# Four of the sixteen tiles of squares summed by TensorE instead of VectorE, in the two bfloat16 contractions of a four-layer kernel

## The reference

```python
z = layernorm(_gn(x), norm_w, norm_b)
left  = sigmoid(z @ w_lgate.T) * mask * (z @ w_left.T)
right = sigmoid(z @ w_rgate.T) * mask * (z @ w_right.T)
out = einsum(left, right) over k, for each of the 64 channels   # bfloat16 operands in layer 0
out = layernorm(out over the 64 channels, onorm_w, onorm_b)
x = x + (out @ w_out.T) * sigmoid(z @ w_ogate.T)
```

## Time and profile before

| | before |
|---|---|
| time, median of 3 runs | 2086.19 us (2081.47 to 2086.61) |
| time of the profiled execution | 2083.57 us |
| its span, first to last instruction | 2081.8 us |
| granted TensorE clock, mean | 0.964 |
| busy share PE / DVE / ACT / POOL | 89% / 81% / 76% / 29% |
| contraction of half 0 in the span | 265.13 to 306.46 us |
| contraction of half 1 in the span | 377.80 to 419.72 us |

### The profile page before, as it was taken

The page is one execution under the profiler, slowest core; times in us unless marked ns, Lnnn a source line. Parts: engine busy times, 40 slices in busy tenths (PEclk is TensorE's granted clock), DMA queues, the critical chain, the costliest instruction groups (busy, mean ns, idle before and its releaser), DMA issues. The chain is left out here.

```text
span 2081.8 us, 44989 instructions
## 1 busy us (share of the span) xinstructions
PE 1857.6 (89%) x14620; PEld 1249.0 (60%) x14620; DVE 1693.1 (81%) x2717; ACT 1585.0 (76%) x2204; POOL 602.0 (29%) x579
## 2 busy tenths in 40 slices
PE   5798979789888999989989899999997989999998
PEld 4324959555422777855632498987552248878554
DVE  6799989989689868778969896988775987777775
ACT  4698969769899657658989884876888976676676
POOL 1001919265200000016500290741871000000655
PEclk8899989999999999999999999999999999999999
DMA  9599938289789838269979984926997994864897
GB/s 395 226 314 298 250 82 242 81 306 358 306 268 332 301 122 295 69 242 384 418 251 313 280 220 127 282 77 252 392 419 250 311 321 165 273 204 152 298 366 316
DMA packets 297398, 549.55 MB, mean 264 GB/s; under 512 B 14768, under 2 KB 170416, under 8 KB 273712
## 3 DMA queue, kind: packets, MB, share of 16 engines
q1 hardware_dynamic: 295680, 538.38, 74.7%
q10 hardware_dynamic: 1584, 9.51, 1.1%
HBM read 371.67 MB, written 176.16 MB: 263 GB/s over the span
## 5 line engine op out<-in xcount | busy, mean ns | idle before, releaser
L1665 POOL TENSOR_TENSOR LR<-LR,sum 128x2048 f32<-128x2048 f32 x30 | 136.6, 4552 | 512.1 <-DVE LR L1458 512.1
L1674 POOL TENSOR_TENSOR LR<-LR 128x512 f32<-128x512 f32 x96 | 136.5, 1444 | 484.7 <-DVE LR L1720 468.9
L697 PE MATMUL bank<-LR,kst 128*128 128x512 f32 x512 | 252.5, 616 | 8.9 <-ACT LR L719 6.6
L897 POOL TENSOR_TENSOR msgs<-sigs,mask_sb 128x256 f32<-128x256 f32 x192 | 129.3, 689 | 393.0 <-ACT sigs L871 389.5
L1554 PEld LDWEIGHTS bank<-kst,LR 128*128 128x128 f32 x1024 | 152.0, 193 | 110.5 <-issue 89.3
L1566 PE MATMUL bank<-LR,wog 128*128 128x512 f16 x768 | 213.8, 388 | 4.8 <-ACT msgs L1621 4.0
L697 PEld LDWEIGHTS bank<-LR,kst 128*128 128x128 f32 x512 | 86.9, 189 | 178.9 <-issue 172.7
L1039 PE MATMUL bank<-LR 128*128 128x256 f32 x768 | 169.6, 383 | 7.0 <-DVE LR L936 4.2
L1554 PE MATMUL bank<-kst,LR 128*128 128x128 f32 x1024 | 161.5, 282 | 15.6 <-ACT sigs L1616 8.6
L1297 PE MATMUL bank<-LR 128*128 128x256 f32 x768 | 166.6, 379 | 7.0 <-DVE LR L936 4.2
L1039 PEld LDWEIGHTS bank<-LR 128*128 128x128 f32 x768 | 146.4, 192 | 27.4 <-DVE LR L936 4.6
(11 more groups left out here) (234 smaller groups left out, 4785.0 us busy)
## 6 DMA issues: line engine op xcount, KB each, us to landing
LR<-XT SPq DMA_DIRECT2D x89, 1024.0 KB, 9.0
XT<-LR SPq DMA_DIRECT2D x47, 1024.0 KB, 8.4
kept<-XH SPq DMA_DIRECT2D x64, 512.0 KB, 6.0
LR<-XH SPq DMA_DIRECT2D x64, 512.0 KB, 6.5
kept<-XHA SPq DMA_DIRECT2D x64, 512.0 KB, 5.0
LR<-XHA SPq DMA_DIRECT2D x64, 512.0 KB, 6.6
OS<-kept SPq DMA_DIRECT2D x12, 2048.0 KB, 8.3
LR<-OS SPq DMA_DIRECT2D x48, 512.0 KB, 10.3
```

The lines of the kernel that those rows point to most:

```text
L697: last = pe.matmul(banks[3][:, u * BANK:(u + 1) * BANK], K(K_MEAN), sq[t % 3][:, u * BANK:(u + 1) * BANK], start=True, stop=True)
L897: pool.tensor_tensor(msg[g], sig[g], mask_sb[:, kt, bass.ds(m, 4)].unsqueeze(1).broadcast_to([P, C, 4]), ALU.mult).then_inc(gates_masked.s, 1)
L1665: pool.tensor_tensor(v, v, token(sum2, c, C), ALU.mult).then_inc(normalized.s, 1)
L1674: pool.tensor_tensor(by_b(x_of(c), q) if end else by_token_cols(x_of(c), q), by_token(gated[t % 4]), by_token_cols(xi[c % len(xi)], q), AL ...
```

## The change

In parts 1, 5, 9 and 13 of each half the squares are added up by PE. Two float32 matmuls of 512 columns with the float32 identity `K(K_IDENT)` sum the two halves of `squares[e % 2]` into one PSUM bank: bank 7 for parts 1 and 5, bank 6 for parts 9 and 13. They stand on PE two parts later, behind channel sum e + 1. The text calls such a pair "pair 1", "pair 5" and so on. DVE no longer adds these parts (eight adds less in each half), but adds each bank to `sum2` once (`add_pe_squares`), ahead of `take_sums`. Square e + 2, which writes the same buffer, waits for the pair now. The column `most_all` of `fold` moves from bank 7 to bank 6, so that bank 7 is free for pairs 1 and 5 in half 0, and pair 9 in half 0 waits until the fold has been read out of bank 6.

```diff
-            most_row, most_all = bank(6)[0:1, 384:384 + P], bank(7)[:, 256:257]
+            most_row, most_all = bank(6)[0:1, 384:384 + P], bank(6)[:, 320:321]
...
+            by_pe = (1, 5, 9, 13)
+
+            def square_bank(ut):
+                return bank(7 - ut)
+
+            def summed_before(e):
+
+                return 2 * len([i for i in range(e) if i not in by_pe]) + (1 if e > 9 else 0)
...
+                def sum_squares(e):
+                    ut, i = parts[e][0], by_pe.index(e)
+                    if half == 0 and i == 2:
+                        pe.wait_ge(weights.s, weights.n + 8)
+                    pe.wait_ge(squares_ready.s, squares_ready.n + e + 1)
+                    for two in range(2):
+                        last = pe.matmul(square_bank(ut), K(K_IDENT), squares[e % 2][:, 2 * two * N:2 * (two + 1) * N],
+                                         start=(i % 2, two) == (0, 0), stop=(i % 2, two) == (1, 1))
+                    last.then_inc(squares_summed.s, 1)
...
                     if e >= 1:
                         sum_channels(e - 1)
+                    if e - 2 in by_pe:
+                        sum_squares(e - 2)
                 sum_channels(15)
...
-                    if e >= 2:
-                        act.wait_ge(summed.s, summed.n + 2 * (e - 1))
+                    if e - 2 in by_pe:
+                        act.wait_ge(squares_summed.s, squares_summed.n + by_pe.index(e - 2) + 1)
+                    elif e >= 2:
+                        act.wait_ge(summed.s, summed.n + summed_before(e - 1))
                     act.activation(by_channels(squares[e % 2][:, :]), result(e), ACT.Square).then_inc(squares_ready.s, 1)
...
+                def add_pe_squares(ut):
+                    dve.wait_ge(squares_summed.s, squares_summed.n + 2 * ut + 2)
+                    dve.wait_ge(summed.s, summed.n + (25 if ut else 14))
+                    dve.tensor_tensor(sum2[:, ut, :], sum2[:, ut, :], square_bank(ut), ALU.add).then_inc(summed.s, 1)
...
-                    if e > 0:
+                    if e > 0 and e - 1 not in by_pe:
                         add_squares(e - 1)
                     if e == 9:
+                        add_pe_squares(0)
                         take_sums(0)
...
+                add_pe_squares(1)
                 take_sums(1)
```

More of the change, by code:

```diff
@@ L213, in build @@
         squares_ready = sem("squares_ready")
+        squares_summed = sem("squares_summed")
         summed = sem("summed")
@@ L1207, in add_squares @@
                         if e or two:
-                            dve.wait_ge(summed.s, summed.n + 2 * e + two)
+                            dve.wait_ge(summed.s, summed.n + summed_before(e) + two)
                         dve.tensor_tensor(sum2[:, ut, :], sum2[:, ut, :],
@@ L1240, in _ @@
                         copy(e)
-                    if e > 0:
+                    if e > 0 and e - 1 not in by_pe:
                         add_squares(e - 1)
                     if e == 9:
+                        add_pe_squares(0)
                         take_sums(0)
                         if half == 1:
-                            dve.wait_ge(summed.s, summed.n + 18)
+                            dve.wait_ge(summed.s, summed.n + 15)
                             dve.wait_ge(sums_taken.s, sums_taken.n + 1)
@@ L1276, in contract_low @@
             advance((contracted, 16), (copied, 8), (copied_v, 8), (channel_sums, 16), (sums_taken, 2),
-                    (squares_ready, 16), (summed, 32))
+                    (squares_ready, 16), (squares_summed, 4), (summed, 26))
             if half == 0:
```

## The result

| | before | after |
|---|---|---|
| time, median of 12 runs each | 2086.4 us (2081.47 to 2089.97) | 2091.55 us (2087.37 to 2095.08) |
| profiled execution, time and span | 2083.57, 2081.8 us | 2087.42, 2085.1 us |
| busy PE / DVE, whole span | 1857.6 / 1693.1 us | 1870.8 / 1686.2 us |
| stage of half 0 | 41.77 us | 44.78 us |
| stage of half 1 | 42.13 us | 42.07 us |

The ratio of the times is 1.0023, with a 95% interval of 1.0012 to 1.0034. That is a small loss, 2.5 to 7 us; the ratio itself lies within the 0.3% taken as no change. A stage is counted here from its first contraction to PE's first matmul of the next stage. The two stages together are 2.95 us longer in the profiled executions.

A forecast was written before the change was run, and what follows sets the result against it. The prediction took DVE to bound both stages before, and a longer chain through the pairs after. Half 0 +2.5 and half 1 +0.7 sum to +3.2 us: 2086.8 or 2089.4, named as 2088.5 us, range 2082 to 2096.

The forecast's parts named there:

- DVE bounds both stages: Kernel before, both halves: DVE busy 3.83 of 4.00 us in the steady part, its ends counting in full.
- Price of a pair, 1.96 us: On PE, two float32 matmuls were taken to last 1.96 us, 1.80 until the next matmul may start.
- The turn, 8.34 us: Four parts of half 1, copy 5 to copy 9: chain through pair 5 takes 8.34 us, against 7.97 before.
- free pairs: The same four parts with pairs that cost nothing: 7.29 us, by copies 5 and 6, squares 5 to 7, adds 7.
- Half 1, +0.7 us: Stage of half 1: longer by +0.6 to +0.8 us, taken as 0.7, with copy 3 staying at about 384.1.
- Half 0, +2.5 us: Stage of half 0: +2.5 us, with the whole 1.8 us of pair 1 going through to copy 5.
- The wait of pair 9 costs nothing: Half 0: the small DVE fold step that pair 9 waits for is done before channel sum 10 is issued.
- The clock: Half 0: pairs 9 and 1 may keep PE at 2.4 GHz; the sum would then be +1.9 us instead of +3.2.
- Sum, +3.2 us: Both stages: 2.5 + 0.7 = +3.2 us, giving 2086.8 from the profiled execution or 2089.4 from the median; 2088.5 named.
- Rival 1: Both stages: pairs hide in PE's gaps, DVE's 8.5 us come out, 2075 or 2077.7 us; chance 0.05.
- Rival 2: Clock stays up in half 0 and pairs start earlier: 0 to +2 us, 2086 to 2088 us; chance 0.25.
- Rival 3: Two or more bare pairs (1, 5, 13 in half 0; 1, 5 in half 1) at half clock: +12 to +18 us; chance 0.14.

The follow-up runs named there:

- pair ahead of the channel sum: Changed kernel with each pair on PE ahead of channel sum e + 1 instead of behind it: half 1 40.11 us, ratio to the kernel before 1.0009.
- the change again: Same instructions as the changed kernel, compared a second time with the kernel before: ratio 1.0011, half 0 42.53 us, half 1 42.56 us.
- pair 1 alone: Kernel before with PE summing only part 1 of half 0: half 0 42.45 us, half 1 42.51 us, one execution.
- parts 9 and 13: Changed kernel with PE summing only parts 9 and 13 in both halves, DVE adding parts 1 and 5: ratio to the kernel before 0.9981.
- pairs twice: Changed kernel with pairs 1 and 5 of half 1 done twice: half 1 46.01 us, one execution.
- own buffers: Changed kernel with the squares of parts 1, 5, 9 and 13 of half 1 in two separate buffers: half 1 41.20 us, one execution.
- half 1 alone: The change made in half 1 only, half 0 as in the kernel before: ratio to the kernel before 0.9993, half 0 40.68 us.
- the two bfloat16 kernels: Changed kernel with the four parts' squares in bfloat16, ratio to the kernel before 0.9987; and all sixteen parts summed by PE in bfloat16, 0.9949.

## Why the prediction was right, step by step

- *DVE bounds both stages.* Right for the kernel before. After the change it no longer does, as said: the adds wait 3.7 us for squares in half 1.
- *Price of a pair, 1.96 us.* Measured 1.88, and 1.98 for pair 9 of half 0. The half rate that the Trainium skill ("Perfetto Trace Analysis", Engine Utilization) gives FP32_LOW_HIGH would be 0.85 us, an estimate; the trace disagrees.
- *The turn, 8.34 us.* 8.12, by the links named. From copy 5 on, the starts in the rows are 1.25, 0.96, 1.06, 0.45, 1.97, 1.09 and 1.34 us apart: the square and the adds give way to their successors 0.08 us earlier each than was counted, and the pair with its hand-over is 0.04 shorter. For free pairs 7.29 was said and 7.21 measured (in bfloat16), but the path is not quite the one named: adds 6 start behind square 6 and run on into adds 7 (394.27, x4, in the rows of the pair ahead of the channel sum), where the prediction had square 7 and then adds 7, with 0.5 us for hand-overs that it doesn't account for. That these two came out alike is luck.
- *Half 1, +0.7 us.* The difference of the profiled executions, -0.07 us, mixes clocks: contraction 2 took 1.91 us in the kernel before and 1.04 in the kernel after. At the same low clock (the change again) it is +0.43 (42.56 against 42.13), with copy 5 at +0.5 (0.6 said) and copy 9 at +0.7 (1.0 said), as the shorter turn has it; the unchanged half 1 of the run with pair 1 alone, also at a low clock, took 42.51, so it may be as little as 0. At full clock "copy 3 stays" is wrong: the adds of part 1 no longer stand ahead of it, and it comes at 4.99 us where the unchanged code has it at 6.09 (run with parts 9 and 13, whose first nine parts of half 1 are as before). Copy 5 is then at +0.0, copy 9 at +0.2, and the stage at an estimated +0.2 (42.13 less the 0.27 us of copy 3 by the clock). The size was too high, the links were right. From copy 15 to `take_sums` it takes 4.77 us in the change again (5.05 in the kernel after, with contraction 15 at half clock) instead of 3.98: the added bank, which was counted, and 0.1 to 0.4 us of pair 13, which was not.
- *Half 0, +2.5 us.* 2.4 to 2.6 at the same clock. The change again, set against the kernel before less the 1.6 us of its fallen clock (an estimate by the stretches above), has the fold's matmuls at +1.7, copy 9 at +2.3 (2.4 said), the first `take_sums` at +3.05 (3.1), copy 15 at +0.3 to +0.5 (0.2), and the end from copy 15 to the last `take_sums` at 6.12 us against 6.27. The +3.0 of the profiled executions holds 0.7 us of a low clock at the start. "The wait of pair 9 costs nothing" is right, but not because the step it asks for is done before: channel sum 10 was issued at 294.45 us, the small DVE step (L388) started at 295.02 and the pair at 295.22; PE idles behind it anyway.
- *The clock.* The idle 3.85 us before channel sum 11 became 1.16, and the clock stayed at 1.00 there, where it had fallen to 0.50: right. That pair 1 would hold it through the fold, given as possible, did not hold in general: in the profiled execution it was 0.50 around contraction 5, in the change again it stayed up. That case was priced at +1.9 us in all and measured +1.19. Of six executions with a float32 pair 1 ahead of the fold it stayed up in three (the change again, pairs twice, pair 1 alone) and fell in three (the kernel after, pair ahead of channel sum, own buffers). The three where it stayed up are those whose half 0 had begun at full clock (contraction 2 at 1.04 us), the three where it fell had begun low (1.46 to 1.89). Of four without a pair 1 it fell in three, two of them begun at full clock, and stayed up in half 1 alone, begun low; in the two bfloat16 kernels, both begun low, it stayed up. So the start does not decide it by itself, and what does is open.
- *Sum, +3.2 us.* 2.95 in the stages, 3.3 in the span; at the same clock 2.4 to 2.6 and 0 to 0.4, so 2.4 to 3.0. Counted to the end of `take_sums`, as the prediction does, the stages are 44.35 and 41.85 us (43.8 and 42.6 said). That the 2.95 lies so near the 3.2 is in part luck: half 0 had 0.7 us of clock too much, half 1 about 0.3 too little. In the span 2.1 us of the 3.3 were lost before half 0 began and 1.7 won back behind half 1, where nothing was changed: scatter between executions, as large as the effect. The median of 12 runs moved 5.15 us, the second comparison gave 1.0011 (2.3 us), so how much of the 5 us beyond the stages is scatter stays open. The middle of the two times added up, 2086.8 and 2089.4, is 2088.1 and not 2088.5.
- *Rival 1*, DVE's time in full, -8.5 us: wrong. It was what "Perfetto Trace Analysis", Identifying the Most-Contended Engine, of the Trainium skill would suggest. The run with all squares in bfloat16 shows a case where the rule holds: with short pairs and no adds left on DVE, relieving it gave 10.6 us. *Rival 2*, 0 to +2 us with the clock up in half 0: the stages of the change again, +1.19, are in its range, but only because the kernel before had lost 1.6 us to its fallen clock there. *Rival 3*, bare pairs at half clock: not seen; all pairs of the profiled execution took 1.88 to 1.98 us. In other runs pair 13 of half 1 did run slower, at 2.15 us (own buffers) and 2.78 (parts 9 and 13).

## What to carry to other kernels

Moving work off the busiest engine pays only what the next chain leaves: write down the chain that runs through the moved step, with its place in every queue, and compare its turn with the old one before counting busy time. The place of the step in the queue can matter more than its size; here the same eight matmuls one step earlier were worth 2 us of the stage of half 1, 42 us long. And when stages of single profiled executions are compared, look at the granted clock inside them: here it alone moved half 0 by up to 2.25 us, as much as the effect. And if the step must be in the chain, make it short first: in bfloat16 the pair costs a third, and then all sixteen parts may go.

## What the runs showed of the hardware

Two float32 matmuls of 128 x 512 with a 128 x 128 identity took 1.88 us at 2.4 GHz, in four records, where two bfloat16 ones took 0.59 to 0.60 (1.03 at 1.2 GHz). Not expected: the same instructions ran half 0 in 42.5 or 44.8 us, 1.5 us of it by whether the clock fell to 0.50 behind the fold's small matmuls and 0.75 by the clock at the start.
